# A 16-token-chunk delta-rule layer with a mixture-of-experts block: projection weights issued by two engines, down weights in six pieces, the third transposed copy of h by ScalarE, and orders in three parts

## What is computed

```python
x = x + conv(ln_c(x))          # conv: q,k = l2norm(silu(t@Wq|Wk)), v = silu(t@Wv), beta = sigmoid(t@Wb)
# per head (12 heads of 16), token by token:
#   u_t = beta_t * (v_t - S^T k_t);  S = S + k_t u_t^T;  o_t = S^T q_t
# conv output = t + o @ Wo
t = to_tokens(x)
h = ln_t(t)
probs = softmax(h @ router_w); top 2 of 8 experts, gates normalised
routed = sum_e gate_e * ((silu(h@w_gate_e) * (h@w_up_e)) @ w_down_e)      # 8 experts of 192
shared = (silu(h@ws_gate) * (h@ws_up)) @ ws_down                          # 768 wide
t = t + alpha*shared + (1-alpha)*routed,  alpha = sigmoid(h@sg_w + sg_b)
```

## Time and profile before

| | us |
|---|---|
| median of 3 runs | 508.37 (507.17 to 508.55) |
| the profiled execution, whole | 509.27 |
| its span, first to last instruction | 507.4 |
| PE, DVE, POOL, ACT busy | 438.0, 431.1, 412.3, 330.8 |

### The profile page before, as it was taken

One profiled execution on the slowest core, in us unless ns is written; L12 is line 12 of the kernel. 1 busy time (PEld: TensorE's weight loads), 2 busy tenths in 40 slices (PEclk: granted clock), 3 DMA queues, 4 the chain that ended last, 5 costly groups with the idle time before them and its releaser, 6 DMA issues.

```text
span 507.4 us, 10651 instructions
## 1 busy us (share of the span) xinstructions
PE 438.0 (86%) x2496; PEld 391.9 (77%) x2496; DVE 431.1 (85%) x2530; ACT 330.8 (65%) x943; POOL 412.3 (81%) x525
## 2 busy tenths in 40 slices
PE   1245146899999999999999999999999998999996
PEld 0233033779898989898989899898989897989996
DVE  2348769999999999999999999999999999997300
ACT  2387224667676767686858686767676757475853
POOL 4169569989898989898989899898989999885341
PEclk9999999999999999999999999999999999999999
DMA  7939733232324232322323232323232323300300
GB/s 204 229 88 162 193 100 89 77 86 67 100 63 101 65 98 69 90 74 80 85 77 91 74 90 68 81 76 85 63 88 71 86 72 79 94 32 0 111 1 16
DMA packets 44686, 44.11 MB, mean 87 GB/s; under 512 B 19856, under 2 KB 36432, under 8 KB 44624
## 3 DMA queue, kind: packets, MB, share of 16 engines
q1 hardware_dynamic: 41488, 41.08, 31.9%
q10 hardware_dynamic: 3136, 2.36, 1.6%
HBM read 37.13 MB, written 6.29 MB: 86 GB/s over the span
## 4 chain that ended last, share of the span: by engine, by line
DVE 64%; PE 14%; SPq 7%; POOL 6%; issue 3%; DMA 3%; ACT 1%; DVEq 0%; POOLq 0%; ACTq 0%
DVE Pr L1143 14%; DVE bank L1147 14%; DVE u L1145 13%; DVE SH L1151 11%; PE bank L417 5%; POOL PQ L779 2%; POOL PQ L786 2%; SPq L272 2%; DVE st L905 2%; SPq L273 2%; PE bank L403 1%; DMA k_scratch<-khl 1%; DMA Wp<-in_L_conv_Wb_dram 1%; PE bank L391 1%; PE bank L393 1%
## 5 line engine op out<-in xcount | busy, mean ns | idle before, releaser
L824 POOL TENSOR_TENSOR hid<-sg,ug 128x192 f32<-128x192 f32 x192 | 112.6, 602 | 39.6 <-ACT ug L607 19.1
L1143 DVE TENSOR_TENSOR Pr<-SH,bank 128x96 f32<-128x96 f32 x512 | 105.8, 250 | 8.9 <-PE bank L352 7.9
L779 POOL TENSOR_TENSOR PQ<-SH,QB 128x768 f32<-128x768 f32 x62 | 112.5, 1837 | 0.4 <-DVE SH L1151 0.3
L1147 DVE TENSOR_TENSOR bank<-bank,u 128x96 f32<-128x96 f32 x512 | 108.6, 260 | 0.0
L786 POOL TENSOR_TENSOR PQ<-PQ 128x768 f32<-128x768 f32 (+2 forms) x93 | 102.9, 1107 | 6.1
L1145 DVE TENSOR_REDUCE u<-Pr 128x6 f32<-128x102 f32 x512 | 107.5, 253 | 0.0
L417 PE MATMUL bank<-Wd,hidT 128*128 128x192 f32 x576 | 106.5, 326 | 0.0
L1151 DVE TENSOR_TENSOR SH<-SH,bank 128x96 f32<-128x96 f32 x512 | 105.5, 250 | 0.0
L417 PEld LDWEIGHTS bank<-Wd,hidT 128*128 128x128 f32 x576 | 96.2, 190 | 0.0
L606 ACT ACTIVATE sg<-bank 128x192 f32<-128x192 f32 x192 | 63.3, 329 | 28.9 <-PE bank L395 20.8
L617 ACT ACTIVATE hidT<-bank 128x512 f32<-128x512 f32 (+1 forms) x80 | 44.6, 557 | 51.4 <-PE bank L403 51.2
(11 more groups left out here) (148 smaller groups left out, 831.0 us busy)
## 6 DMA issues: line engine op xcount, KB each, us to landing
QB<-q_scratch SPq DMA_DIRECT2D x64, 384.0 KB
k_scratch<-khl SPq DMA_DIRECT2D x64, 48.0 KB, 1.9
KR<-k_scratch SPq DMA_DIRECT2D x32, 96.0 KB, 2.4
q_scratch<-qn SPq DMA_DIRECT2D x64, 24.0 KB, 1.7
Wd<-in_L_ffn_w_down_dram SPq DMA_DIRECT2D x1, 1152.0 KB, 19.9
out_dram<-xT SPq DMA_DIRECT2D x1, 896.0 KB, 4.2
Wlo_unsplit<-in_L_ffn_w_gate_dram ACTq DMA_DIRECT2D x1, 768.0 KB, 5.3
Wlo_unsplit<-in_L_ffn_w_up_dram ACTq DMA_DIRECT2D x1, 768.0 KB, 8.8
```

The source lines that it names most:

```text
L779: tt(PQ[:, at * BR * HP:(at + n) * BR * HP].rearrange("p (i b h) d -> p i b (h d)", i=n, b=BR), SH[:, lo:lo + n].rearrange("p i b h d -> p ...
L824: tt(hid[:, r * H:(r + 1) * H], sg[:, m % RING], ug[:, m % RING], ALU.mult).then_inc(s_hid, 1)
L1143: v = each(lambda br: count(tt(Pr[:, br, i, :, 0:D], prev[:, br], KB[:, br], ALU.mult)), Sb)
L1147: v = each(lambda br: count(tt(KB[:, br], KB[:, br], u[:, i % 2, br].unsqueeze(2).to_broadcast([P, HP, D]), ALU.mult)), v)
```

## The change

It has four parts. (1) `load_projection` (new) issues three DMAs of one weight; SP keeps Wq and Wk, ACT issues Wv and Wb as its first instructions. (2) Wd is loaded by `load_down(i)` in six pieces of three 128-row blocks (288 KB each), issued by SP at the end of step 0 (three) and of step 1 (three); `load_later` loads only x. (3) PE no longer makes the second copy of the low channels. ACT copies them itself: `A_hT` has three copies in place of one, `Fa_hT` five in place of two, and `h2T` has no second copy. DVE's `Fa_split` and `A_low` become two instructions each, of 128 columns, the second on 64 partitions; the lower halves of `loT` and `hlo` are set to zero once by two new POOL memsets, for which PE and DVE wait before anything else. (4) The order lists of PE, ACT, POOL and DVE exist three times: c < 1, 1 <= c < 16, c >= 16.

```diff
+        def load_projection(eng, w, lo, hi):
+            eng.dma_start(Wp0[:, lo:hi], w[0:C0, :]).then_inc(s_wp, 16)
+            eng.dma_start(Wp1[0:C1, lo:hi], w[C0:C, :]).then_inc(s_wp, 16)
+            eng.dma_start(Wp1[C1:P, lo:hi], w[C0:C, :]).then_inc(s_wp, 16)
...
+                load_projection(sp, Wq, 0, C)
+                load_projection(sp, Wk, C, 2 * C)
...
             def load_later():
                 load_x(1, FIRST * T, L)
+            def load_down(i):
                 ke = E * H // P
-                sp.dma_start(Wd[:, 0:ke, :], w_down.rearrange("e h c -> (e h) c").rearrange("(k p) c -> p k c", p=P)).then_inc(s_wd, 16)
-                sp.dma_start(Wd[:, ke:KT, :], ws_down.rearrange("(k p) c -> p k c", p=P)).then_inc(s_wd, 16)
+                if i < 4:
+                    sp.dma_start(Wd[:, 3 * i:3 * i + 3, :], w_down.rearrange("e h c -> (e h) c").rearrange("(k p) c -> p k c", p=P)[:, 3 * i:3 * i + 3]
+                                 ).then_inc(s_wd, 16)
+                else:
+                    k = 3 * i - ke
+                    sp.dma_start(Wd[:, 3 * i:3 * i + 3, :], ws_down.rearrange("(k p) c -> p k c", p=P)[:, k:k + 3]).then_inc(s_wd, 16)
...
                 if c == -1:
                     load_later()
+                for i in range(KT // 3):
+                    once(c, i // 3, load_down, i)
...
-                turn(bA, h)
-                mm(bA[C1:P, P:2 * P], h[:, C0:C], ident[:, :], start=True, stop=True).then_inc(s_hTp, 1)
+                turn(bA, h).then_inc(s_hTp, 1)
...
-                f(hhi[:, :], bA[:, 0:2 * P], ACT.Copy).then_inc(s_hT, 1)
+                f(hhi[:, 0:P], bA[:, 0:P], ACT.Copy)
+                f(hhi[0:C1, P:2 * P], bA[0:C1, P:2 * P], ACT.Copy)
+                f(hhi[C1:P, P:2 * P], bA[0:C1, P:2 * P], ACT.Copy).then_inc(s_hT, 1)
...
-                f(h2T[:, :], bFa[:, 0:2 * P], ACT.Copy)
-                f(hiT[:, p], bFa[:, 0:2 * P], ACT.Copy).then_inc(s_h2T, 1)
+                f(hiT[:, p, 0:P], bFa[:, 0:P], ACT.Copy)
+                f(hiT[0:C1, p, P:2 * P], bFa[0:C1, P:2 * P], ACT.Copy)
+                f(hiT[C1:P, p, P:2 * P], bFa[0:C1, P:2 * P], ACT.Copy)
+                f(h2T[:, 0:P], bFa[:, 0:P], ACT.Copy)
+                f(h2T[0:C1, P:2 * P], bFa[0:C1, P:2 * P], ACT.Copy).then_inc(s_h2T, 1)
...
+            pool.memset(loT[:, :, :].bitcast(F32), 0.0).then_inc(s_low0, 1)
+            pool.memset(hlo[:, :].bitcast(F32), 0.0).then_inc(s_low0, 1)
...
-                tt(hlo[:, :], bA[:, 0:2 * P], hhi[:, :].bitcast(F32), ALU.subtract).then_inc(s_hlo, 1)
+                tt(hlo[:, 0:P], bA[:, 0:P], hhi[:, 0:P].bitcast(F32), ALU.subtract)
+                tt(hlo[0:C1, P:2 * P], bA[0:C1, P:2 * P], hhi[0:C1, P:2 * P].bitcast(F32), ALU.subtract).then_inc(s_hlo, 1)
...
+                    elif c < NC:
+                        at(11, 2, A_low)
...
+                        at(31, 1, A_vT)
...
+                        at(44, -1, Fa_split)
...
+            dve.wait_ge(s_low0, 2)
+            pe.wait_ge(s_low0, 2)
```

More of the change, by code:

```diff
@@ L368, in Fa_h @@
                 pe.wait_ge(s_h2, f + 1)
[L369 to L372 removed]
+                turn(bFa, h2).then_inc(s_h2Tp, 1)
             def Fa_logits(f, p):
@@ L455, in step @@
-                at(1, fill, 1)
-                at(-1, Fb_up, 2)
-                at(3, A_h)
-                at(-2, Fb_turn, 4)
-                at(-1, Fb_up, 3)
-                at(1, fill, 2)
-                at(-2, Fb_down, 3)
-                at(-1, Fb_up, 4)
-                at(3, A_vb)
-                at(3, A_qk)
+                if c < 1:
+                    at(0, fill, 3)
+                    at(3, A_x)
+                    at(0, fill, 4)
+                    at(0, fill, 5)
+                    at(0, fill, 6)
+                    at(0, fill, 7)
+                    at(1, fill, 0)
+                    at(1, fill, 1)
+                    at(3, A_h)
+                    at(1, fill, 2)
+                    at(3, A_vb)
+                    at(3, A_qk)
+                elif c < NC:
+                    at(0, fill, 3)
+                    at(-3, Fb_down, 4)
+                    at(-2, Fb_up, 5)
+                    at(-2, Fb_up, 6)
+                    at(-1, Fa_o)
+                    at(0, fill, 4)
+                    at(3, A_x)
+                    at(-3, Fc_out)
+                    at(-2, Fb_turn, 0)
+                    at(-1, Fa_y)
+                    at(-2, Fb_up, 7)
+                    at(-2, Fb_up, 8)
+                    at(-2, Fb_turn, 1)
+                    at(0, fill, 5)
+                    at(-2, Fb_up, 9)
+                    at(-1, Fa_h)
+                    at(-2, Fb_up, 10)
+                    at(0, fill, 6)
+                    at(-2, Fb_down, 0)
+                    at(-1, Fa_logits)
+                    at(-2, Fb_turn, 2)
+                    at(-2, Fb_up, 11)
+                    at(-1, Fb_up, 0)
+                    at(0, fill, 7)
+                    at(-2, Fb_down, 1)
+                    at(-2, Fb_turn, 3)
+                    at(-2, Fb_down, 2)
+                    at(1, fill, 0)
+                    at(-1, Fb_up, 1)
+                    at(-1, Fb_up, 2)
+                    at(-2, Fb_turn, 4)
+                    at(3, A_h)
+                    at(1, fill, 1)
+                    at(-2, Fb_down, 3)
+                    at(1, fill, 2)
+                    at(-1, Fb_up, 3)
+                    at(-1, Fb_up, 4)
+                    at(3, A_vb)
+                    at(3, A_qk)
+                else:
+                    at(-3, Fb_down, 4)
+                    at(-2, Fb_up, 5)
+                    at(-1, Fa_o)
+                    at(-2, Fb_up, 6)
+                    at(-2, Fb_turn, 0)
+                    at(-1, Fa_y)
+                    at(-2, Fb_up, 7)
+                    at(-2, Fb_up, 8)
+                    at(-2, Fb_turn, 1)
+                    at(-3, Fc_out)
+                    at(-2, Fb_up, 9)
+                    at(-2, Fb_up, 10)
+                    at(-1, Fa_h)
+                    at(-2, Fb_down, 0)
+                    at(-2, Fb_turn, 2)
+                    at(-2, Fb_up, 11)
+                    at(-1, Fa_logits)
+                    at(-2, Fb_down, 1)
+                    at(-1, Fb_up, 0)
+                    at(-2, Fb_turn, 3)
+                    at(-2, Fb_down, 2)
+                    at(-1, Fb_up, 1)
+                    at(-1, Fb_up, 2)
+                    at(-2, Fb_turn, 4)
+                    at(-2, Fb_down, 3)
+                    at(-1, Fb_up, 3)
+                    at(-1, Fb_up, 4)
@@ L708, in _ @@
+            load_projection(act, Wv, 2 * C, 3 * C)
+            load_projection(act, Wb, 3 * C, 3 * C + NH)
             nc.scalar.preload_act_table_set(SILU)
```

399 lines of the change are left out of this document (228 added, 171 removed).

## The result

| | before | after |
|---|---|---|
| median of the runs, us | 507.77 (4 runs) | 501.31 (500.72 to 502.54, 4 runs) |
| ratio | | 0.9876, 95% interval 0.9849 to 0.9903 |
| the profiled execution, its span | 509.27, 507.4 | 500.72, 499.0 |

The change is faster by 6.3 us (4.9 to 7.7, the interval times 508). The forecast was a gain of 10.3 us and 498.1 us; 501.31 lies in the range (494.0 to 503.5) but outside the likeliest case's own (496 to 500.5), close to rival A (501.8). The two profiled executions are 8.55 apart, 2.1 more than the medians: that of before is 1.5 over its median, that of after 0.6 under its own.

A forecast was written before the change was run, and what follows sets the result against it. DVE was taken to bound the full chunks, with its time before and between chunks and PE's tail also counting. Gains 7.4 + 2.3 + 1.3 + 1.2 - 1.9 = 10.3 us gave a median of 498.1, range 494.0 to 503.5.

The forecast's parts named there:

- likeliest case: The forecast itself, a gain of 10.3 us to a median of 498.1, within 496 to 500.5; chance 0.60.
- rival A: DVE's idle gap between chunks 0 and 1 only half closes, k waiting behind x; 3.7 us stay, 501.8; chance 0.12.
- the hole: DVE idle between chunks 0 and 1 for 7.41 us, because SP's Wd loads held back chunk 1's k writes.
- Wd, "Gain 7.4": Between chunks 0 and 1: moving Wd later in six pieces lets DVE pass without idling; 7.4 us gained.
- Start, "Gain 2.3": Before chunk 0: low part of h^T starts 2.8 us earlier, less 0.5 for a weight split; 2.3 us gained.
- Waits for ACT and POOL, "Gain 1.3": DVE's wait for ACT in chunk 0 shrinks by 0.6 us and for POOL in chunk 1 by 0.7.
- Two instructions for one, "1.9 lost": DVE's cut subtractions in the full chunks: 29 extra instructions at 0.065 us each; 1.9 us lost.
- Middle lists, "Cost 0": Full chunks: PE's fill 7 moves later but keeps 1 us of room before DVE needs it; cost 0.
- The end, "Gain 1.2": Around DVE's last transpose: PE gets there 0.8 us sooner and has 0.4 less behind it; 1.2 us gained.
- C: Wd's last three pieces land late in chunk 2, so PE and then DVE lose 5 us or so; 503; chance 0.04.
- D: Weights, memsets and both small waits turn out well and the lists close what is left; 494.5; chance 0.10.
- E: SP's queue or POOL's new list keeps start and hole; only extra instructions show; 509 to 510; chance 0.03.

The follow-up runs named there:

- part 2 alone: The kernel before with only Wd loaded in six pieces at the end of steps 0 and 1; 501.99 us, ratio 0.9886.
- a_wd_whole: The changed kernel with Wd again in two DMAs behind the rest of x in step -1; 508.18 us, ratio 0.9999.
- part 1 alone: The kernel before with only the Wv and Wb loads issued by ACT; 508.51 us, ratio 1.0019.
- a_pe_copy: The changed kernel with PE making the second copy again and DVE's subtractions whole; memsets, waits and lists stay; 501.19 us, ratio 0.9865.
- b_no_lists: The changed kernel with the order lists of before, parts 1, 2 and 3 staying; 503.09 us, ratio 0.9916.

## Why the prediction was right and wrong

- **What bounds it, and the hole: right in kind.** Wd ahead of k's writes made it; part 2 alone gives all that the change gives.
- **The number.** Of 10.3 us forecast 6.3 came. In the two profiled executions the sum fell short by 1.9 (8.40 of 10.3): 2.2 were missing at the start of chunk 1 (8.09 of 10.3), and from there on 0.3 came where I had 0. The other 2.1 are what these two executions are further apart than the medians. That the number landed beside rival A's is in part luck: of A's 3.7 us, 2.3 showed.
- **Wd, "Gain 7.4": the step that failed, on top of an earlier start.** Alone the term is nearly right: 7.15 us in the trace and 5.8 by the ratios, because chunk 0 ends as late as before. With the start moved I still took the whole because "of 2,880 KB issued from 37.8 on, 1,728 are Wd and no longer compete". What remained, x with QB's 1,536 KB ahead of it, which that count leaves out, was enough: x landed at 54.6, where the lower bound had it at 54.9, KR went out at 55.36, and 2.33 us stayed. That bound (3.7 stay, chunk 1 at 60.8; it was 59.28) is rival A, to which I gave 0.12. It rested on the rows, a transfer issued at 38.32 that takes 18.9 us; the full gain only on a count of bytes.
- **The sum: terms that end at the same event were added.** Start, ACT's wait and the hole all end where KR of chunk 1 arrives. Wd alone moved that point by 7.15 us (67.37 to 60.22), the whole change by 8.09; of the 2.9 that I had added for the start and the wait for ACT 0.94 arrived in these executions, and by the ratios nothing (a_wd_whole 0.9999).
- **Start, "Gain 2.3": right up to k's writes, wrong behind them.** Statistics at 9.59 (forecast 9.5), low part at 14.13 (14.6), writes issued 2.8 earlier. But I looked at no queue there: the up weights stood ahead, and 1.14 of the 2.8 were lost by KR's loads in this execution, and all 4.2 in part 1 alone. Chunk 0 of the six kernels with the start of the change began between 32.58 and 36.07; in before at 34.50.
- **The two-engine rule.** The Trainium skill (DMA: Bandwidth & Descriptors, "Issuing engines are not separate DMA queues") lets only sequencer time be saved. That was saved and was all of the wait: in part 1 alone DVE no longer waits for Wb, which held it until 15.04 before. The rule decided nothing here: in the change the weights were there when DVE came to them at 11.58, and how long before, no wait shows.
- **Waits for ACT and POOL, "Gain 1.3": 1.6.** In chunk 0 DVE's work up to the end is 1.09 shorter (24.37 against 25.46, the times from the first Pr to the end of the chunk), the 1.50 for ACT less a wait for a fill that grew from 0.44 to 0.88; in chunk 1 0.54. The first of the two ended in the hole.
- **Two instructions for one, "1.9 lost": right.** 0.065 us each, shown by 26.49 and by 26.76 with twice as many; 1.58 from first to last otok. My line through the rows gives only 0.05 to 0.06 an instruction, 1.5 to 1.7 in all; I used 0.065 without a row for it, and that it came out is luck in the last digit.
- **Middle lists, "Cost 0", and ACT's five copies: right.** Fill 7 has 1.6 us of room (forecast 1).
- **The end, "Gain 1.2": right.** 1.35: PE takes up the transpose at 459.58, 0.43 behind it instead of 1.32. How it splits depends on the order: in a_pe_copy, with the new lists, PE's product is 0.54 and the lists 0.8; in b_no_lists, without the product, the lists are 1.1 and the product 0.2.
- **Rivals.** C: Wd's pieces landed 8.6 us (w_down) and 9.3 us (ws_down) after issue, by the medians, and nobody waited. D and E did not come. What I named as a sign, under 1 us idle at chunk 1, read 2.33: wrong case.

## What to carry to other kernels

Before gains are added, write beside each the event at which it ends; those that end at one arrival (here KR of the next chunk) give the largest, not the sum, and a bound by the queue's traffic comes on top. Follow a small latency-critical DMA past everything issued before it on any engine: in these kernels the megabytes ahead set when it lands, and issuing it earlier only made its own row longer. After each such reordering look for the next small write that is now behind the moved load.
